# Pairwise feature products: the last load cut by columns, a quarter of each row moved in DMAs of 125 and 3 partitions

## What is computed

```python
xw = jnp.einsum('bfe,ed->bfd', x, W)
return xw[:, i_idx, :] * x[:, j_idx, :]
```

## Time and profile before

| | |
|---|---|
| median of three runs | 651.27 us (651.10 to 652.02) |
| the profiled execution | 650.9 us |
| its span, first to last instruction | 649.1 us |
| VectorE busy | 568.8 us, 88% of the span |
| TensorE busy | 161.0 us, 25% |
| ScalarE busy | 139.7 us, 22% |
| moved by DMA | 277.01 MB, 427 GB/s over the span |

### The profile page before, as it was taken

The page is one execution under the profiler, slowest core; times in us unless marked ns, Lnnn a source line. Parts: engine busy times, 40 slices in busy tenths (PEclk is TensorE's granted clock), DMA queues, the critical chain, the costliest instruction groups (busy, mean ns, idle before and its releaser), DMA issues.

```text
span 649.1 us, 2595 instructions
## 1 busy us (share of the span) xinstructions
PE 161.0 (25%) x776; PEld 81.5 (13%) x776; DVE 568.8 (88%) x528; ACT 139.7 (22%) x259; POOL 0.7 (0%) x6
## 2 busy tenths in 40 slices
PE   5614060603206032060420604114060411400000
PEld 3302030301103011030110302002030200200000
DVE  3999999899689996899968899999999989999940
ACT  4513050504105031050310504023050502301000
POOL 0000000000000000000000000000000000000000
PEclk9958575755757557566575756658585665755555
DMA  8999999999999999999999999999999999999996
GB/s 366 445 417 451 424 421 441 424 423 432 422 438 428 436 426 422 446 420 442 423 432 433 442 423 445 427 427 444 427 444 425 428 443 422 442 432 425 446 425 293
DMA packets 8524, 277.01 MB, mean 427 GB/s; under 512 B 1088, under 2 KB 1088, under 8 KB 1088
## 3 DMA queue, kind: packets, MB, share of 16 engines
q1 hardware_dynamic: 7632, 268.44, 96.1%
q10 hardware_dynamic: 880, 8.42, 3.1%
HBM read 16.81 MB, written 260.05 MB: 427 GB/s over the span
## 4 chain that ended last, share of the span: by engine, by line
DMA 54%; DVE 39%; issue 2%; PE 0%; DVEq 0%; ACTq 0%; ACT 0%
DMA out_dram<-out_ring 53%; DVE out_ring L272 39%; DMA W_sb<-in_W_dram 1%; PE xwT_ps L154 0%; DVEq L60 0%; ACTq L239 0%; ACT xw_first L206 0%; DVEq L268 0%
## 5 line engine op out<-in xcount | busy, mean ns | idle before, releaser
L272 DVE TENSOR_TENSOR out_ring<-xw_rest,x_sb 128x832 f32<-128x832 f32 (+21 forms) x384 | 323.2, 916 | 15.2 <-DMA out_dram<-out_ring 15.2
L272 DVE TENSOR_TENSOR out_ring<-xw_first,x_sb 128x1984 f32<-128x1984 f32 (+2 forms) x144 | 247.1, 1781 | 39.5 <-DMA out_dram<-out_ring 28.7
L173 PE MATMUL xwT_ps<-xT_sb,W_sb 64*64 64x512 f32 x252 | 84.1, 751 | 392.3 <-ACT xT_sb L212 392.3
L236 ACT COPY xw_rest<-xw_ps 128x512 f32<-128x512 f32 x48 | 28.1, 585 | 429.0 <-DVE out_ring L272 399.9
L218 ACT COPY xwT_sb<-xwT_ps 64x512 f32<-64x512 f32 x126 | 73.3, 581 | 10.6 <-PE xwT_ps L173 9.9
L173 PEld LDWEIGHTS xwT_ps<-xT_sb,W_sb 64*64 64x64 f32 x252 | 14.4, 156 | 405.3 <-ACT xT_sb L212 396.1
L183 PE MATMUL xw_ps<-identity,xwT_sb 128*128 128x128 f32 x252 | 48.4, 322 | 28.3 <-ACT xwT_sb L218 28.3
L146 PE MATMUL xT_ps<-identity,x_sb 128*128 128x128 f32 x256 | 44.8, 306 | 6.0 <-DMA x_sb<-in_x_dram 6.0
L183 PEld LDWEIGHTS xw_ps<-identity,xwT_sb 128*128 128x128 f32 x252 | 31.0, 159 | 92.9 <-ACT xwT_sb L218 77.9
L212 ACT COPY xT_sb<-xT_ps 128x512 f32<-128x512 f32 x63 | 37.2, 591 | 1.8 <-PE xT_ps L146 0.9
L146 PEld LDWEIGHTS xT_ps<-identity,x_sb 128*128 128x128 f32 x256 | 36.0, 162 | 7.0 <-issue 6.0
(11 more groups left out here) (1 smaller groups left out, 0.1 us busy)
## 6 DMA issues: line engine op xcount, KB each, us to landing
out_dram<-out_ring SPq DMA_DIRECT2D x32, 5280.0 KB, 26.1
out_dram<-out_ring SPq DMA_DIRECT2D x16, 5312.0 KB, 25.4
x_sb<-in_x_dram SPq DMA_DIRECT2D x3, 2048.0 KB, 16.0
x_sb<-in_x_dram ACTq DMA_DIRECT2D x3, 2048.0 KB, 22.9
x_sb<-in_x_dram SPq DMA_DIRECT2D x2, 1024.0 KB, 6.2
x_sb<-in_x_dram ACTq DMA_DIRECT2D x2, 1024.0 KB, 27.8
W_sb<-in_W_dram ACTq DMA_DIRECT2D x2, 16.0 KB, 6.1
```

Of the source, the lines that this page charges most:

```text
L173: nc.tensor.matmul(xwT_ps[s % 2][odd][rows, :, :], W_sb[rows, :], xT_sb[s % 2][rows, :, :], start=True, stop=True).then_inc(projected[odd], 1)
L236: nc.scalar.copy(xw_of(t, g), xw_ps[s % 2][:]).then_inc(xw_copied, 1)
L272: last = nc.vector.tensor_tensor(slot[:, place:place + n, :], one.to_broadcast([LANES, n, E]), x_sb[buf][:, r, j:j + n, :], ALU.mult)
```

## The change

The last load (load 7) goes as three DMAs instead of one. The first moves the first 3072 elements (12 KB) of each partition's 4096, on all 128 partitions. The second moves the other 1024 elements (4 KB) on partitions 0 to 124, the third the same columns on partitions 125 to 127. All three are issued by ScalarE at the place of the old one, in that order, and raise the same semaphore by 16 each; the two waits for load 7 count 64 in place of 32. No other load, no store and no computation is touched.

```diff
--- before.py
+++ after.py
@@ -14,6 +14,8 @@
 CUTS = (0, 165, 330, 496)
 CHUNKS = len(CUTS) - 1
 ALIGN = 256
+ASIDE = 1024
+ASIDE_ROWS = 125
 
 
 def pair_pieces(F):
@@ -128,6 +130,10 @@
             for slot in range(CHUNKS):
                 sp.wait_ge(stored[slot], 16 * TILES)
 
+        def landings(load):
+
+            return 16 * (load // XBUFS + (3 if load == LOADS - 1 else 1))
+
 
         groups = [(t, g) for t in range(TILES) for g in range(GROUPS)][1:]
 
@@ -140,7 +146,7 @@
                 load, r = divmod(t, ROWS)
                 buf = load % XBUFS
                 if f == 0 and r < len(x_landed[buf]):
-                    pe.wait_ge(x_landed[buf][r], 16 * (load // XBUFS + 1))
+                    pe.wait_ge(x_landed[buf][r], landings(load))
                 for m in range(n):
                     two = x_sb[buf][:, r, f + 2 * m:f + 2 * m + 2, :].rearrange("p f e -> p (f e)")
                     last = nc.tensor.transpose(to[:, m, :], two, identity[:])
@@ -230,8 +236,16 @@
                         if buf == 0:
                             for r in range(ROWS):
                                 act.dma_start(x_sb[0][:, r], x_loads[done + XBUFS, :, r]).then_inc(x_landed[0][r], 16)
+                        elif done + XBUFS < LOADS - 1:
+                            act.dma_start(x_sb[buf][:], x_loads[done + XBUFS]).then_inc(x_landed[buf][0], 16)
                         else:
-                            act.dma_start(x_sb[buf][:], x_loads[done + XBUFS]).then_inc(x_landed[buf][0], 16)
+
+                            to = x_sb[buf][:].rearrange("p r f e -> p (r f e)")
+                            run = x_loads[done + XBUFS].rearrange("p r f e -> p (r f e)")
+                            cut = ROWS * F * E - ASIDE
+                            act.dma_start(to[:, 0:cut], run[:, 0:cut]).then_inc(x_landed[buf][0], 16)
+                            for few in (slice(0, ASIDE_ROWS), slice(ASIDE_ROWS, LANES)):
+                                act.dma_start(to[few, cut:], run[few, cut:]).then_inc(x_landed[buf][0], 16)
                 act.wait_ge(turned_back, s + 1)
                 nc.scalar.copy(xw_of(t, g), xw_ps[s % 2][:]).then_inc(xw_copied, 1)
 
@@ -263,7 +277,7 @@
                     slot = out_ring[c][:].rearrange("p (q e) -> p q e", e=E)
                     for i, j, n, place in chunks[c]:
                         if i == 0 and r < len(x_landed[buf]):
-                            dve.wait_ge(x_landed[buf][r], 16 * (load // XBUFS + 1))
+                            dve.wait_ge(x_landed[buf][r], landings(load))
                         if j == i + 1 and t == 0 and i in (0, FIRST):
                             dve.wait_ge(xw_copied, i // FIRST + 1)
                         elif j == i + 1 and i % GROUP == 0:
```

## The result

The changed kernel takes 653.85 us (median of seven runs, 652.79 to 654.31) against 651.49 for the kernel before in the same comparison (650.41 to 652.02). The ratio is 1.0033, with a 95% interval of 1.0024 to 1.0043: slower, by 2.2 us, 1.6 to 2.8. The forecast of 650.2 was wrong, and the range to 653.4 ended 0.45 us short. What came is the first rival: late engines were among the five.

The account below looks back on a forecast made before the run. It took the latest DMA engine's store packets as the bound: profiled 650.9 less 1.1 gives 649.8, and the median 651.27 less 1.1 gives 650.2, with issues and waits costing nothing; range for all cases 649.6 to 653.4 us.

Parts of the forecast that it names:

- the first rival: Load 7's 25-row shares hit an engine ending after 646.6: 2.57 to 2.72 us more there, 652.4 to 653.9; chance 0.29.
- The bound: Stores set the pace; the latest of sixteen DMA engines, not the mean, bounds the kernel, its last packet ending at 648.1.
- The division: Load 7's 125 small rows go in equal shares, 25 on each of five engines; the three odd rows separately.
- the relief: Load 7's large DMA carries 12 KB a row instead of 16, sparing each engine 32.8 KB, 1.21 us.
- the surplus: Five engines carry 25 rows of 4 KB, 3.78 us, less 1.21: 2.57 us more than before.
- The second price of the relief: From VectorE's release stages, a load costs the latest engine 5.0 to 5.35 us, a quarter of one 1.25 to 1.34.
- if the two latest engines are among the eleven: At the tail, both latest engines get no 25-row share and end at 646.9; chance taken 0.68 given five engines.
- late engines are neighbours: End times in blocks suggest engines lying together share delays; the first five would spare both latest in 10 of 15 places.
- The signs: Tail and queue: last packet ends about 646.9, fewer engines through by 643.5, 1,016 packets; wrong if last starts after 646.6.
- the middle block: Nine engines in the tail whose last packets end between 643.52 and 645.08, leaving 3 to 4.6 us unused.
- The issues: ScalarE issues three DMAs instead of one, 0.37 us each, so the copies behind come 0.74 us later.
- The cover: ScalarE finishes its copies at 326.79, 9.9 us before VectorE reads the first, so later issues cost nothing.

Follow-up runs that it names:

- the probes: Kernel before plus one DMA of 51, 68 or 85 rows of 4 KB, 17 rows on each of three, four or five engines: 651.77, 652.61, 653.63 us.
- 126 and 127 rows: Changed kernel with its small DMAs on 126 and 2, or 127 and 1, partitions instead of 125 and 3: 651.39 us (0.9998) and 664.51 us (1.0196).
- the probe of three engines: Kernel before plus one DMA of 51 rows of 4 KB into buffer 0 after its last use: 651.77 us, ratio 1.0000.

## Why the prediction was wrong

- **The bound** was right: the latest engine's packets, not the mean. Adding to three engines costs nothing, to five 2.1 us (the probes), and taking 32.8 KB off all gives 1.3.
- **The division** was right: five equal shares of 25 and three of one, shown by the counts in the queue line, by the packets followed one by one, and by the counts for 126 and 127 rows.
- **The sizes** were right: 1.21 for the relief (1.3 measured, 0.7 to 1.9), 2.57 for the surplus (2.65 in the chain's piece). The second price of the relief, 1.25 to 1.34, left out the stage right behind load 7, 38.23 us, which is also longer than the others; the sum did not use it.
- **The step that failed** is "if the two latest engines are among the eleven", and the chance of 0.68 put on it. In its place the runs showed both of the latest among the five: the last two engines to end, at 649.9 and 651.5, carry 25 small rows each, and the probes cost nothing on three engines and 2.1 us on five. The count alone had given 0.46. What raised it was the guess that late engines are neighbours, which the first five would spare in 10 of 15 places, 0.67; the 0.68 taken lies above both. Whether the two are neighbours no run here shows, as none shows numbers; if they are, they lie inside the five. Nothing in the rows said where they lay, and the argument turned a lack of knowledge into two chances in three.
- **The range** then cut off the upper half of the first rival, 652.4 to 653.9, at 653.4. The result, 653.85, lies in that half. The mechanism and the place of the rival were as they came out, and nearly its price: the last packet ends at 651.5 in the profiled execution, 0.7 past the 650.8 of its far end.
- **The signs** named ahead: the last packet starts at 649.9, past 646.6, as the text said of a wrong forecast, and the 1,016 packets came. "Fewer engines through by 643.5" did not: it was ten in place of four, most likely because the relief brings engines of the middle block under that mark.
- **The rules of the Trainium skill**, page DMA: Bandwidth & Descriptors: what it says of the number of engines (section on the increment by 16) agrees with every line of ScalarE's queue here: 125 on 5, 126 on 14, 127 on 1, 51 on 3, 85 on 5. Its sentence that engines 7 and 15 are usually the slower ones (Latency and other measured facts) stands there with a best guess that ties it to DMAs issued by GpSimd, and the kernel before issues all of its own from SyncE and ScalarE: it was no ground for the forecast. By the numbers of its section on the increment by 16, which no run here shows, the two latest engines of this kernel are among the lowest five. Its rule to put a multiple of 16 outermost (Rules for kernel authors) is borne out here where the few engines are late ones; the probe of three engines and the DMA of 126 rows show where breaking it costs nothing.
- **The issues** were priced at 0.37 us each and took 0.94 and 1.34 us; the copies behind came 2.34 us late instead of 0.74. The trace before had shown it at load 4, which goes as two DMAs: the second took 1.29 us (in ns: shortest, median, longest).

```profile
L232 ACTq DMA_DIRECT2D x_sb<-in_x_dram x2: 362/824/1286, 80.8 to 81.2; - x2
```

- **The cover** that was named, 9.9 us, was enough. The waits for 64 cost nothing, as said: in the whole trace VectorE waits for no load.

## What to carry to other kernels

In a kernel like this one, whose stores fill all DMA engines, a transfer has a price for each engine, and the end is set by the engine with the least slack: before bytes are moved from engine to engine, find out whether late ones are hit, with a probe that loads k engines for a known time, and repeat it over several runs. The number of packets in ScalarE's queue line told on how many engines a DMA ran (its rows plus one count for each), and the row count decided it: 126 rows were harmless here, 125 cost 2.2 us by late engines, 127 cost 13 by the hold of ScalarE. A time that meets a forecast does not show the mechanism: the trace of 127 rows had another. Where the rows do not say which resource is late, count the places and leave it at that.

## What the runs showed of the hardware that was not expected

On ScalarE a DMA issued right behind a load takes long to issue: 0.36 us for the first and 0.93 to 1.48 us for each of the small ones behind it, whether on few engines or on all sixteen, and 1.29 for the second half of load 4. That points to the place in the row and not to the form: the probes' DMAs, of the same 4 KB rows and issued alone, took 0.36 to 0.53 us. Far from all this is the last DMA behind the one of 127 rows on one engine: a single row, it kept ScalarE's sequencer for 43.4 us (the line's instructions, shortest, median and longest in ns):

```profile
L248 ACTq DMA_DIRECT2D x_sb<-in_x_dram x2: 1286/22359/43432, 317.2 to 318.5; - x2
```

What holds the sequencer was not tried. Why two of the five engines are late was not tried either, and it stays open.
